# A two-layer LSTM graph kernel: layer 1's gate table projected around step 0's gates, and the opening's x rows gathered without a pause

## What is computed

```
def step(carry, x_t):
    h, c = carry
    g = x_t @ wih.T + h @ whh.T + b
    i, f, gg, o = jnp.split(g, 4, axis=-1)
    c = jax.nn.sigmoid(f) * c + jax.nn.sigmoid(i) * jnp.tanh(gg)
    h = jax.nn.sigmoid(o) * jnp.tanh(c)
    return ((h, c), None)

def _sage_conv(x, src, wih, whh, bih, bhh, wl, bl, wr):
    msgs = x[src].reshape(n, d, c)
    aggr = _lstm_last(jnp.swapaxes(msgs, 0, 1), wih, whh, bih, bhh)
    return aggr @ wl.T + bl + x @ wr.T
```

## Time and profile before

| | us |
|---|---|
| runs (three): median | 528.24 |
| runs: lowest, highest | 525.88, 529.69 |
| the profiled execution's own time | 524.9 |
| its span, first to last instruction | 523.1 |
| mean granted clock of PE | 0.979 |

### The profile page before, as it was taken

One profiled execution on the slowest core, in us unless ns is written; L12 is line 12 of the kernel. 1 busy time (PEld: TensorE's weight loads), 2 busy tenths in 40 slices (PEclk: granted clock), 3 DMA queues, 4 the chain that ended last, 5 costly groups with the idle time before them and its releaser, 6 DMA issues.

```text
span 523.1 us, 10333 instructions
## 1 busy us (share of the span) xinstructions
PE 481.5 (92%) x3599; PEld 361.0 (69%) x3599; DVE 415.0 (79%) x1134; ACT 334.4 (64%) x851; POOL 351.6 (67%) x485
## 2 busy tenths in 40 slices
PE   8499999999999979899999999999999987979785
PEld 3378887888888865688888888889855443434343
DVE  3569989989999975888888888889879866565655
ACT  1466877677767754677676777677657554555452
POOL 6658877887787832788888878877046556555660
PEclk9799999999999999999999999999999998979899
DMA  4855565555655632555556555655021111111110
GB/s 159 335 161 163 163 179 155 158 168 167 174 155 162 179 97 100 162 142 162 161 158 167 162 143 164 163 161 159 22 86 36 45 37 40 41 40 37 41 40 26
DMA packets 25907, 66.32 MB, mean 127 GB/s; under 512 B 6278, under 2 KB 10174, under 8 KB 25728
## 3 DMA queue, kind: packets, MB, share of 16 engines
q0 software_dynamic: 18048, 55.85, 37.8%
q1 hardware_dynamic: 6720, 8.89, 5.4%
q10 hardware_dynamic: 1088, 0.92, 0.6%
HBM read 62.48 MB, written 3.16 MB: 125 GB/s over the span
## 4 chain that ended last, share of the span: by engine, by line
PE 50%; DVE 18%; DMA 15%; ACT 8%; issue 6%; POOL 2%; DVEq 0%; ACTq 0%; POOLq 0%
PE gates L1240 20%; DMA edge_rows<-msg_table,msg_index 12%; PE gates L1233 7%; PE gates L1185 5%; PE work L1240 5%; PE work L1162 5%; DVE prod_fc L901 3%; DMA code<-in_x,src_steps 3%; DVE h_full L872 3%; DVE prod_ig L903 3%; DVE msg_full L1087 2%; ACT act_if L606 2%; ACT h_hi L596 2%; ACT msg_full L743 2%; PE work L1233 2%
## 5 line engine op out<-in xcount | busy, mean ns | idle before, releaser
L524 POOL DMA_INDIRECT rows<-gate_table,src_steps x192 | 198.6, 1034 | 53.8 <-POOL pause L522 51.3
L537 POOL DMA_INDIRECT edge_rows<-msg_table,msg_index x76 | 76.8, 1011 | 67.6 <-ACT msg_full L743 25.9
L1240 PE MATMUL gates<-h_hi,whh_hi 128*128 128x256 f16 x396 | 100.7, 273 | 4.2 <-ACT h_hi L596 2.6
L1240 PE MATMUL gates<-h_hi,whh_lo 128*128 128x256 f16 x396 | 100.4, 273 | 0.0
L600 ACT ACTIVATE act_if<-gates 128x512 f32<-128x512 f32 x96 | 57.4, 598 | 50.5 <-PE gates L1240 50.4
L522 POOL MEMSET pause<- 128x256 f32 x199 | 66.9, 336 | 33.6 <-DMA gate_table<-rows 17.3
L1240 PE MATMUL gates<-h_lo,whh_hi 128*128 128x256 f16 x396 | 85.5, 274 | 0.4 <-DVE h_lo L885 0.4
L1233 PE MATMUL gates<-ident,rows 128*128 128x128 f32 x584 | 79.7, 273 | 3.6 <-issue 3.4
L1233 PEld LDWEIGHTS gates<-ident,rows 128*128 128x128 f32 x584 | 67.0, 141 | 7.5 <-issue 4.6
L901 DVE TENSOR_TENSOR prod_fc<-act_if,cell 128x256 f32<-128x256 f32 x128 | 53.8, 421 | 20.4 <-ACT act_if L600 9.6
L1077 DVE TENSOR_SCALAR rows<-node_iota,dst_f 128x512 f16<-128x512 f16 x132 | 43.2, 361 | 28.4 <-ACT msg_full L743 28.3
(11 more groups left out here) (180 smaller groups left out, 1000.4 us busy)
## 6 DMA issues: line engine op xcount, KB each, us to landing
rows<-gate_table,src_steps POOLq DMA_INDIRECT x192, 3.5
gate_table<-rows SPq DMA_DIRECT2D x8, 256.0 KB, 2.0
src_direct<-direct_rows SPq DMA_DIRECT2D x1, 2048.0 KB, 7.7
edge_rows<-msg_table,msg_index POOLq DMA_INDIRECT x76, 2.5
code<-code_table SPq DMA_DIRECT2D x6, 160.0 KB, 3.8
msg_table<-table_sb SPq DMA_DIRECT2D x4, 192.0 KB, 1.9
code<-code_table SPq DMA_DIRECT2D x5, 128.0 KB, 3.5
whhT<-turned_whh SPq DMA_DIRECT2D x2, 256.0 KB, 7.7
```

The source lines that it names most:

```text
L524: pool.indirect_dma_start(target, None, table, bass.IndirectOffsetOnAxis(src_steps[:, t, k:k + 1], axis=0)).then_inc(landing(l, t, k)[0], 16)
L537: pool.indirect_dma_start(edge_rows[:, c % 2, n, :], None, msg_rows, bass.IndirectOffsetOnAxis(msg_index[:, pool_first(c) + n:pool_first(c ...
L1240: mm = pe.matmul(gate_place(t, h, gate), w[:, gate * P:(gate + 1) * P], state[:, h, :], start=(opens and opens_bank(t, gate) and n == 0), ...
```

## The change

It has two parts.

1. Between the layers PE first picks x for step 0, projects tiles 0 and 1, computes step 0's gates, projects tiles 2 and 3, and picks x for step 1 last. For that the four tiles have other PSUM banks: tiles 0 and 1 lie in `work` banks 2 and 3, tiles 2 and 3 in `work` banks 0 and 1, none in a bank of `gates`; the x picked for step 1 shares `work` banks 2 and 3. ACT copies step 0's x and tile 0, then does step 0, and behind its last tanh tile 3 and step 1's x. DVE likewise: step 0's x, tile 1, step 0, tile 2, step 1's x. PE has new waits for copied tiles ahead of the picks for steps 1 and 2; those of `first_gates` go.
2. In the opening, the eight gathers of x rows have no pause in front of them. The gathers of table rows keep theirs.

Which tiles are computed, and what each gather brings, is the same.

```diff
-                      [gate_bank[0], gate_bank[1], gate_bank[2], work[:, 2, :]]]
+                      [work[:, 2, :], work[:, 3, :], work[:, 0, :], work[:, 1, :]]]
...
-        pick_pair = {(1, 1): (gate_bank[3], work[:, 3, :])}
+        pick_pair = {(1, 1): (work[:, 2, :], work[:, 3, :])}
...
-                    if at > 0:
+                    if not by_x_row:
                         pool.memset(pause[:, :], 0.0).then_inc(paused, 1)
-                        pool.wait_ge(paused, at)
+                        pool.wait_ge(paused, by_rows.index((l, t)) * K + k + 1)
...
                     tanh_of_cell(1, now)
                     if l == 0 and t == 0:
                         take_x(0, 1)
+                    elif t == 0:
+                        table_part(1, 3)
+                        take_x(1, 1)
...
-                    if 1 in tabled:
-                        if 0 in tabled:
-                            act.wait_ge(table_stored, 16 * K)
-                        table_part(1, 0)
-                        table_part(1, 3)
                     take_x(1, 0)
-                    take_x(1, 1)
+                    act.wait_ge(table_stored, 16 * K)
+                    table_part(1, 0)
...
-                    if 1 in tabled:
-                        if 0 in tabled:
-                            dve.wait_ge(table_stored, 16 * K)
-                        table_part(1, 1)
-                        table_part(1, 2)
                     take_x(1, 0)
-                    take_x(1, 1)
+                    dve.wait_ge(table_stored, 16 * K)
+                    table_part(1, 1)
                     dve.wait_ge(code_loaded, 16 * BLOCKS)
...
                 if l == 0:
                     take_x(0, 1)
                     build_onehot(0, range(2, K))
+                else:
+                    table_part(1, 2)
+                    take_x(1, 1)
...
-                    else:
-                        if 1 in tabled:
-                            pe.wait_ge(table_taken[0], len(tabled) * K // 2)
-                            pe.wait_ge(table_taken[1], len(tabled) * K // 2)
-                        gathered_taken(1, h)
+                    elif h == 0:
+                        gathered_taken(1, 0)
...
                     elif t + 1 < T and MODES[l][t + 1] == "P":
+                        if (l, t) == (1, 1):
+                            pe.wait_ge(table_taken[0], K)
+                            pe.wait_ge(table_taken[1], K)
                         gather_x(l, t + 1)
...
-                    if 1 in tabled:
-                        pe.wait_ge(o_ready[1], T)
-                        for k in range(K):
-                            add_bias(1, k, first=True)
-                            project(1, h1T, k, last=True).then_inc(projected, 1)
                     pe.wait_ge(centred_ready, 1)
                     gather_x(1, 0)
+                    pe.wait_ge(o_ready[1], T)
+                    for k in (0, 1):
+                        add_bias(1, k, first=True)
+                        project(1, h1T, k, last=True).then_inc(projected, 1)
+                    first_gates(1)
+                    for k in (2, 3):
+                        add_bias(1, k, first=True)
+                        project(1, h1T, k, last=True).then_inc(projected, 1)
+                    pe.wait_ge(table_taken[0], K // 2 + 1)
+                    pe.wait_ge(table_taken[1], K // 2 + 1)
                     gather_x(1, 1)
-                    first_gates(1)
```

## The result

| | before | after |
|---|---|---|
| median, us (20 runs each) | 527.07 | 530.88 |
| lowest to highest, us | 524.15 to 530.12 | 528.72 to 535.5 |
| profiled execution: own time, span | 524.9, 523.1 | 531.44, 529.6 |
| first-half tanh of step 32 of layer 0 | 194.61 | 195.74 |
| from there to the same tanh in layer 1 | 178.82 | 183.09 |

The ratio is 1.0075, with a 95% interval of 1.0054 to 1.0095: some 4.0 us slower. That is a real loss, since the interval keeps clear of 1, and yet it lies within the 1% that the prediction set as its bound between "slower" and "same": the case that came is the one it gave 0.35, not the likelier 0.59. The forecast was 6.3 slower, 534.5 us.

The account below looks back on a forecast made before the run. It took POOL's gather stream to end layer 0 and nearly end layer 1, close to the step path. Layer 1 +7.1 and opening −0.8 gave +6.3: 531.2 us profiled, plus 3.3 for timed runs, 534.5; range 527.5 to 537.5.

Parts of the forecast that it names:

- slower: Whole kernel: time rises by more than one per cent, 5.3 us; chance 0.59.
- same: Whole kernel: time stays within one per cent, 5.3 us, of before; chance 0.35.
- The stream has only 1.1 us to spare: End of layer 1, step 32: a gather stream starting over 1.1 us late ends the layer late, unless it catches up.
- The gathers start 8.5 us later: Between the layers: tiles 2 and 3 are stored late, so POOL's layer 1 gathers start 8.5 us later.
- the 0.3 that I gave back for the builds: Start of layer 1's gathers: the six pick builds no longer run beside the first gathers, so 0.3 us comes back.
- The step path comes out 1.9 us later: Between the layers: step 0's gates 3.65 us earlier, but late x for step 1 leaves the steps 1.9 us later.
- that rule: PE ahead of step 1: an idle PE falls to half clock, putting the step path at about +4.9, not +1.9.
- The opening, −0.8: Start of the kernel: x gathers without pauses let half a gather more start before POOL's long landing wait, gaining 0.8 us.
- Rival 1: Opening: two more gathers get under way, layer 0 ends 3.1 us earlier; total +4.0, 532.2 us; chance 0.11.
- Rival 2: Layer 1: the stream makes up its lag and the step path decides; +1.1, 529.3 us; chance 0.12.
- Rival 3: Between the layers: step 1's x is in time and the stream catches up, gaining 3.65 plus 0.8; 523.8 us; chance 0.03.
- Rival 4: First gathers of layer 1: pick builds had held POOL 3.60 us, which comes back; +3.0, 531.2 us; chance 0.05.

Follow-up runs that it names:

- after again: The changed kernel, unchanged, profiled a second time: one execution, 528.44 us.
- the run with 13 pauses: Kernel before with 13 extra chained pauses on POOL ahead of layer 1's first gather, nothing else moved: ratio 1.0057 to before.
- the two lags of 5.74 and 10.86: Kernel before with 13 and with 26 extra pauses ahead of layer 1's first gather, starting it that many us later: ratios 1.0057 and 1.0194.
- the mended change: Changed kernel with ACT's and DVE's late copies of tiles 2 and 3 and step 1's x put inside step 0: ratio 1.0005 to before.
- the run with step 1's x late: Kernel before with step 1's x picked behind step 0's gates and copied behind step 0, stream on time: ratio 1.0047 to before.

## Why the prediction was right or wrong

**The order of the work: right.** Step 0's gates 3.65 us earlier; tiles 2 and 3 and step 1's x behind step 0 on DVE and ACT; PE idle ahead of step 1's input, though for 2.75 us and not 4; the table late; PE waiting for rows at step 32, with a stream no faster than before (20.1 and 19.3 per twelve). Each of these stands in the rows above. Waits before steps 30 and 31 were forecast too and didn't come in this profile, where the lead at step 31 was still 6.71; in after again PE waited 0.84 before step 31. That there were so few follows from the next point.

**"The stream has only 1.1 us to spare": this is the term that failed.** It was 7.58 − 6.42 = 1.16 in the one profile that I had, and right for it. But the step path repeats to 0.05 us and the stream doesn't: 157.8 and 157.3 in two other profiles, so 3.1 and 3.7 to spare, and 3.3 by the run with 13 pauses. The rows showed a hint that I read past: the windows of twelve ran from 19.36 to 21.05 within that one layer. Where a margin is the difference of two long sums, one execution gives one draw of it.

**"The gathers start 8.5 us later": nearly right, 7.73.** The builds alone took 2.46 and not 3.60, which brings all of step 0 and the copies behind it 1.14 earlier. From the end of tile 2's copy (211.63) to the pause (214.37) it was 2.74, not 2.42, which gives 0.32 back. With 7.73 and a spare of 3.4 the loss is 4.3, and 4.27 is what the profile shows. Predicted was 7.1: of the 2.8 too much, some 2.2 is the spare and 0.8 the start, less the 0.3 that I gave back for the builds. Against the timed 530.88 the forecast of 534.5 is 3.6 too high: 1.2 of that is its base, 528.24 from three runs where twenty have 527.07, and the rest is what the sum had too much.

**"The step path comes out 1.9 us later": at step 1, 2.24 with the half clock and 0.65 without.** Step 1's input began 1.2 earlier than reckoned, by the builds, which makes 0.7 of the 1.9, and that is what two of three profiles show. In the third, after, 12 matmuls and the pick took 2.52 + 2.12 = 4.64 where I had 3.04, 1.6 more, all at half clock or on the way back. The prediction weighed that rule (the Trainium skill, "TensorE: Matmul & The Clock Gate", "What's actually happening") and left it out of the sum because it wouldn't decide. The clock did fall to 0.50 once and stayed at 1.00 twice behind the same idle time, and it didn't decide. By the tanh of step 31 the three stand 2.65, 2.08 and, after again, 3.54 behind before's (in after 372.60 − 195.74 = 176.86 against 368.82 − 194.61 = 174.21), but by then PE had also waited for late rows of the table, by step 5 in all three, which the prediction hadn't seen. At the true spare the two paths of after lie only 183.09 − (178.82 + 2.65) = 1.6 apart, not 5: I set the clock aside for a margin that wasn't there.

**The opening, −0.8: +0.15, between −1.3 and +1.6.** The timed runs don't exclude −0.8, but its mechanism isn't in the traces. Five or six table gathers had been launched ahead of POOL's long wait, and the seventh starts at 33.4 to 34.6 either way. So the number launched before it didn't set that time; what did, no run shows. I had named zero as the lower end, and then taken half a gather without a row for it.

**The rivals.** Rival 1's number, +4.0, is what came out, by luck: its opening gained none of the 3.1 us that it asked for. Rival 2, the stream making up its lag, is refuted by the two lags of 5.74 and 10.86, whose difference came through whole; what looked like catching up is a spare of 3.3. Rival 3 fell as its paragraph said, by the order of the two engines; the mended change shows that even with the order put right the table decides. Rival 4 had the builds hold POOL for their whole 3.60 us. It fails by the size: POOL's three intervals between gathers took 5.00 beside the builds and 219.73 − 214.95 = 4.78 without, 0.2 more. It was DVE that lost, 3.60 us for six builds against 2.46 (1.1 more). Gathers aren't needed for that: in the run with 13 pauses, where only those memsets stood beside the builds, the six took 3.23. The Trainium skill's "SBUF — State Buffer", "Who interferes with whom", says that whichever of the two engines issues first keeps the shared pair and blocks the other, so it allows this direction as well as the one that the prediction took from it; a block of a whole instruction no row here shows.

**What stays open.** Why engines stand without a releaser when the pauses go; why layer 0's end, and the stretch behind layer 1 (148.2 to 153.8 in the profiles), scatter by several microseconds in one kernel; and why the run with step 1's x late lost 4.2 in its profile and 2.5 timed. If its clock falls in some executions and not in others, as the changed kernel's did, that would explain about 1.5 us of it, but only one execution was profiled.

## What to carry to other kernels

When two nearly equal paths end a stage, measure the spare between them from several executions, or with a deliberate delay on one of them as above; a single trace gives a figure that can be off threefold. Work moved out of the front of a critical step lands on the inputs of the next one: follow each copy to its new place on its engine, and ask both what needs it next and which transfer waits for it. And before you reorder the expensive pieces, look for cheap ones (here six builds nobody needed for 150 us) that stand in front of the critical instruction.

## What the runs showed of the hardware

- Without a memset of 0.33 us and a wait for it between gathers on POOL the changed kernel takes 588.5 us instead of some 530, and with one of 0.22 us before is 14.6 us slower than with one of 0.33. ACT's longest wait in layer 0 with no releaser that the profile knows is then 9.5 us without pauses (`act_if`) and 2.6 with the narrow one.
- Behind the same 2.75 us without a matmul, in the same order of instructions, PE was granted 0.50 for about three microseconds in one profile and 1.00 throughout in two. Behind 3.92 us it had 0.50 and behind 1.51 us 1.00, in one profile each.
- DVE's builds and POOL's gathers and pauses slow each other unequally: +1.1 us in 2.5 on DVE, 0.2 in 4.8 on POOL. Beside POOL's memsets alone it was +0.8 on DVE.
